# Weights asked for later, and a planner with one wire and other durations, in a three-layer decoder kernel

## The reference, cut to what matters

```
x = x + local(layernorm(x))             # 16 heads; a token sees its 7 nearest neighbours
x = x + cross(layernorm(x), ctx_1024)   # 16 heads; softmax over 120 context rows
h = layernorm(x)
h = h + causal(rmsnorm(h, n1_w))        # 16 heads, causal mask
h = h + silu(rmsnorm(h, n2_w) @ up.T) @ down.T * (sum of the 2 largest gate shares, normalised)
x = x + h
```

## Time and profile before

| what | value |
|---|---|
| median of 3 runs | 3523.06 us (3519.29 to 3523.43) |
| profiled execution | 3525.48 us, its span 3523.7 us |
| mean granted TensorE clock | 0.986 of full |
| TensorE, VectorE, GpSimd, ScalarE busy | 97%, 76%, 71%, 52% of the span |
| DMA queue of SP | 217.44 MB, 18.0% of 16 engines' span |

### The profile page before, as it was taken

The page is one execution under the profiler, slowest core; times in us unless marked ns, Lnnn a source line. Parts: engine busy times, 40 slices in busy tenths (PEclk is TensorE's granted clock), DMA queues, the critical chain, the costliest instruction groups (busy, mean ns, idle before and its releaser), DMA issues.

```text
span 3523.7 us, 91852 instructions
## 1 busy us (share of the span) xinstructions
PE 3421.1 (97%) x36229; PEld 2775.1 (79%) x36229; DVE 2680.4 (76%) x5867; ACT 1829.9 (52%) x4241; POOL 2499.1 (71%) x3160
## 2 busy tenths in 40 slices
PE   5699999999999999999999999999999999999997
PEld 4477888888888888888888888888888888888876
DVE  5687787787787787787787787787787787787763
ACT  2345545545545545545545545545545545545542
POOL 5677777777777777777777777777777777777731
PEclk8799999999999999999999999999999999999998
DMA  5111221121121221121121221221121121121200
GB/s 169 61 52 47 69 77 47 69 77 47 69 77 47 69 77 47 69 77 47 69 77 47 69 77 46 69 77 47 69 77 47 69 77 47 69 77 47 69 8 10
DMA packets 90149, 223.31 MB, mean 63 GB/s; under 512 B 9286, under 2 KB 56706, under 8 KB 73346
## 3 DMA queue, kind: packets, MB, share of 16 engines
q1 hardware_dynamic: 89730, 217.44, 18.0%
HBM read 164.92 MB, written 50.39 MB: 61 GB/s over the span
## 4 chain that ended last, share of the span: by engine, by line
PE 95%; DVE 2%; ACT 1%; POOL 1%; DMA 0%; issue 0%; SPq 0%; DVEq 0%; ACTq 0%
PE ps L892 13%; PE ps L901 13%; PE ps L763 11%; PE ps L870 10%; PE ps L819 10%; PE ps L741 9%; PE ps L797 9%; PE ps L842 8%; PE ps L769 4%; PE ps L721 3%; PE ps L791 1%; PE ps L808 1%; PE ps L856 1%; ACT prob L1006 1%; DVE nmax L1328 1%; DMA y<-in_ctx 0%
## 5 line engine op out<-in xcount | busy, mean ns | idle before, releaser
L1162 POOL TENSOR_TENSOR chunks<-v_windows,xT 128x560 f32<-128x560 f32 (+1 forms) x384 | 880.0, 2302 | 85.5 <-DVE xT L1303 76.6
L1328 DVE TENSOR_REDUCE nmax<-ps 128x4 f32<-128x480 f32 (+2 forms) x1280 | 776.8, 671 | 178.0 <-PE ps L797 178.0
L1006 ACT ACTIVATE prob<-ps 128x256 f32<-128x256 f32 (+2 forms) x1536 | 670.5, 557 | 436.0 <-PE ps L819 436.0
L1157 POOL TENSOR_TENSOR chunks<-rest,k_windows 128x512 f32<-128x512 f32 (+1 forms) x384 | 552.2, 1454 | 366.7 <-DMA k_windows<-passed_on 291.7
L1282 DVE TENSOR_REDUCE held<-chunks 128x80 f32<-128x560 f32 (+1 forms) x384 | 294.4, 767 | 303.3 <-POOL chunks L1162 297.0
L892 PE MATMUL ps<-xT,w_up 128*128 128x256 f32 x2048 | 485.2, 385 | 1.6 <-ACT xT L959 1.6
L901 PE MATMUL ps<-w_down,held 128*128 128x256 f32 x2048 | 459.0, 382 | 1.9 <-DVE held L1381 1.6
L901 PEld LDWEIGHTS ps<-w_down,held 128*128 128x128 f32 x2048 | 383.9, 190 | 59.7 <-DVE held L1381 1.9
L892 PEld LDWEIGHTS ps<-xT,w_up 128*128 128x128 f32 x2048 | 375.2, 191 | 70.5 <-issue 20.2
L959 ACT COPY xT<-ps 128x512 f32<-128x512 f32 x256 | 153.1, 598 | 355.1 <-PE ps L721 355.1
L1174 POOL TENSOR_SCALAR_AFFINE_SELECT prob<-prob 128x512 f32<-128x512 f32 x512 | 310.9, 641 | 35.9 <-ACT prob L1006 35.8
(11 more groups left out here) (150 smaller groups left out, 6719.6 us busy)
## 6 DMA issues: line engine op xcount, KB each, us to landing
k_windows<-passed_on SPq DMA_DIRECT2D x64, 1024.0 KB, 5.0
v_windows<-passed_on SPq DMA_DIRECT2D x64, 1024.0 KB, 5.0
x<-in_x SPq DMA_DIRECT2D x64, 256.0 KB, 2.9
passed_on<-rest SPq DMA_DIRECT2D x64, 256.0 KB, 2.0
passed_on<-held SPq DMA_DIRECT2D x64, 256.0 KB, 3.4
out<-x SPq DMA_DIRECT2D x64, 256.0 KB, 2.2
y<-in_ctx SPq DMA_DIRECT2D x64, 120.0 KB, 2.8
held<-nmaxT SPq DMA_DIRECT2D x256, 8.0 KB
```

The costliest lines, as they stand in the source:

```text
L1006: last = nc.scalar.activation(prob_pair(seq, L, m)[0:keys, :, r, col:col + qs], of_pair, ACT.Exp, scale=SCALE)
L1157: last = nc.gpsimd.tensor_tensor(chunk_of(c).rearrange("p (j d) -> p j d", d=D), q_row, window("k", (b + first) * D, (D, n), (1, D)), ALU. ...
L1162: last = nc.gpsimd.tensor_tensor(chunk_of(c).rearrange("p (h i j) -> p h i j", i=HD, j=WINDOW), window("v", b * D + first * HD, (HD, n), ( ...
L1328: nc.vector.tensor_reduce(of_heads[:, ms[0]:ms[-1] + 1, :, r], src, AX_X, ALU.max, negate=True).then_inc(emptied[b], 1)
```

## The change

- `setup_parts` gives transfers their bytes (`kb`), and the plan keeps one `wire` on which transfers follow each other at 330 KB/us, each seen 1.1 us (`LANDING`) after it has passed.
- Many durations and lags in the plan are other numbers (ACT and DVE lag 0.15 to 0.2, `derive bias` 4.6 to 7.0, `window_max` 1.68 to 1.38, and so on). TensorE's parts take up to twice as long in the plan after a pause of over 1.5 (`warmth`). A PSUM bank is empty 0.24 after its reader, whichever engine that is.
- `BEHIND`: group 3 is offered to SP only when the first sequence's k fetch has been issued, group 4 when its v fetch has been.
- GpSimd's masks become a part of the plan (`constants`), with the same instructions.
- `EARLY` and `EARLY_ON_DVE` would let VectorE do some of the multiplications of the first sequences. `EARLY` is 0, so no part uses it, and no such instruction is emitted.

`POSITION`, `SHIFTED`, `FILLING`, `LOOKS` and all emitted instructions stay. The core of the diff:

```
-LAG = {"PE": 0.21, "ACT": 0.15, "DVE": 0.15, "POOL": 0.1}
+LAG = {"SP": 1.1, "PE": 0.21, "ACT": 0.2, "DVE": 0.2, "POOL": 0.1}
-DIVIDE, REJOIN, CHANGE = 0.1, 0.2, 0.11
+DIVIDE, REJOIN, CHANGE = 0.1, 0.22, 0.15
+EASY_REJOIN = 0.13
+WIRE = 330.0
+LANDING = 1.1
+COOLS_AFTER, WARMS_IN = 1.5, 3.4
+EMPTIED = 0.24
+EARLY = 0
+BEHIND = {("weights", (3,), "SP"): ("fetch", ("k",), "SP", 0), ("weights", (4,), "SP"): ("fetch", ("v",), "SP", 0)}
...
-             for n, (busy, lag) in enumerate(((2.0, 5.0), (2.0, 6.0), (3.0, 10.0), (4.5, 12.0), (5.5, 18.0)))]
-    part("zeros", (), "SP", 0.6, [], lag=2.5)
+             for n, (busy, kb) in enumerate(((1.9, 768), (1.9, 768), (2.8, 1280), (3.5, 1040), (4.0, 2060)))]
+    part("zeros", (), "SP", 1.2, [], lag=LANDING, kb=60)
+    constants = part("constants", (), "POOL", 5.1, [])
...
-    part("derive", ("bias",), "DVE", 4.6, [loads[3], ("derive", ("half",), "DVE")])
+    part("derive", ("bias",), "DVE", 7.0, [loads[3], ("derive", ("half",), "DVE")])
     part("derive", ("scale",), "DVE", 4.3, [loads[3], loads[4]])
...
-    loaded = part("load", (), "SP", 2 * DMA_ISSUE, [], [("lane", ())], lag=3.2)
+    loaded = part("load", (), "SP", 2 * DMA_ISSUE, [], [("lane", ())], lag=LANDING, kb=376)
-                    sent[w] = part("send", (w,), "SP", DMA_ISSUE, [rows[w]], lag=1.9)
+                    sent[w] = part("send", (w,), "SP", DMA_ISSUE, [rows[w]], lag=LANDING, kb=256)
-                fetched[w] = part("fetch", (w,), "SP", DMA_ISSUE, [sent[w]], [(w + "_window", ())], lag=4.8)
+                fetched[w] = part("fetch", (w,), "SP", DMA_ISSUE, [sent[w]], [(w + "_window", ())], lag=LANDING, kb=1024)
...
+                        if now - stopped > COOLS_AFTER:
+                            warmth = 0.0
+                        cold = min(2 * (end - now), WARMS_IN - warmth)
+                        warmth += cold
+                        end += cold / 2
+                        stopped = end
+                    landed = end
+                    if p.kb:
+                        wire = landed = max(wire, end) + p.kb / WIRE
...
+                    j = released.get((n, i))
+                    if j is not None:
+                        missing[0, j] -= 1
+                        if not missing[0, j]:
+                            offer(0, j)
```

More of the change, by code:

```diff
@@ L62, in score_units @@
     return fills if layer == CROSS else fills + [tuple((g, 1) for g in range(4))]
-Part = namedtuple("Part", "name args engine busy lag after takes gives")
-LAG = {"PE": 0.21, "ACT": 0.15, "DVE": 0.15, "POOL": 0.1}
+Part = namedtuple("Part", "name args engine busy lag after takes gives kb", defaults=(0,))
+LAG = {"SP": 1.1, "PE": 0.21, "ACT": 0.2, "DVE": 0.2, "POOL": 0.1}
 DMA_ISSUE = 0.42
@@ L162, in sequence_parts, with part @@
     needs.update({("up", m): needs["up", 0] for m in range(1, 4)})
-    def part(name, args, engine, busy, after, takes=(), gives=(), lag=None):
+    def part(name, args, engine, busy, after, takes=(), gives=(), lag=None, kb=0):
         first = engine in ("PE", "SP")
@@ L231, in sequence_parts @@
                 held.append(a)
-                a = part(*step, "ACT", 2.0 if u < 2 else 2.3, [a] + first[1::2], (), [("quad", step)])
+                a = part(*step, "ACT", 1.95 if u < 2 else 2.15, [a] + first[1::2], (), [("quad", step)])
                 held.append(a)
@@ L299, in __init__, with engine_of @@
         at = {p[:3]: i for i, p in enumerate(parts)}
+        early = {i: EARLY_ON_DVE[p[:2]] for i, p in enumerate(parts) if p[:2] in EARLY_ON_DVE and p.engine == "POOL"}
+        released = {(who[3], at[who[:3]]): at[what] for what, who in BEHIND.items()}
+        def engine_of(n, i):
+            return "DVE" if n < EARLY and i in early else parts[i].engine
         followers = defaultdict(list)
@@ L323, in offer @@
         def offer(n, i):
-            if parts[i].engine != "PE":
-                ready[parts[i].engine].append((n + due[i] + 0.001 * n, n, i))
-                ready[parts[i].engine].sort()
+            e = engine_of(n, i)
+            if e != "PE":
+                ready[e].append((n + due[i] + 0.001 * n, n, i))
+                ready[e].sort()
+        for i in released.values():
+            missing[0, i] += 1
         for n, i in todo:
-            if not parts[i].after:
+            if not missing[n, i]:
                 offer(n, i)
@@ L366, in __init__ @@
         idle, events, now = set(engines), {}, 0.0
+        wire, stopped, warmth = 0.0, 0.0, 0.0
         while True:
@@ L385, in __init__ @@
                     self.order[e].append((p.name, n, p.args))
-                    end = now + p.busy
+                    busy = early[i] if e == "DVE" and i in early else p.busy
+                    end = now + busy
                     if e == "PE":
@@ L1051, in _ @@
[L1051 to L1065, removed]
@@ L1273, in _ @@
                         w, b, first, n = CHUNKS[c]
-                        dve.wait_ge(multiplied[s], reached["multiplied", "window_times", seq, (c,)])
+                        if seq < EARLY and ("window_times", (c,)) in EARLY_ON_DVE:
+                            dve.wait_ge(doubled[s], reached["doubled", "window_times", seq, (c,)])
+                        else:
+                            dve.wait_ge(multiplied[s], reached["multiplied", "window_times", seq, (c,)])
                         if w == "k":
```

151 lines of the change are left out of this document (94 added, 57 removed).

## The result

The changed kernel took 3541.52 us, the median of 4 runs (3539.04 to 3548.05), against 3523.24 (4 runs) for the kernel before. The ratio is 1.0047, 95% interval 1.0034 to 1.0059: slower by 0.5%, where 3511 was forecast, and outside the range. The profiled execution is the longest of the four, 3548.05 us with a span of 3546.3, so its 22.6 us over the span before overstate the median's 18.3.

The account below looks back on a forecast made before the run. TensorE was taken as the bound, saturated in the middle, with losses in the ramp set by the first sequence's local attention. First sequence -10 and rest of the ramp -2 gave -12 us: 3511 us against the median, range 3490 to 3531.

Parts of the forecast that it names:

- Start of the first k chunk: First sequence's first k chunk, at 31.58 before: starts near 27.5 through earlier `project_rows` and send, -4 us.
- rival 1: Ramp: wire and VectorE give the gain back, sends land no earlier; 3521 us, chance 0.20.
- Chunk stalls: First sequence's k chunks: two of three GpSimd stalls go, the one of `bias` stays, -5.5 us.
- Softmax: First sequence, from last k chunk to first v chunk: a little less lost, -0.5 us, bounds -1.4 and +3.
- scale: VectorE's 7.2 us weight scaling, expected at k's end or in the softmax: 0 us, bounds -3.7 and +3.5.
- the first sequence: Sum of the terms up to the first sequence's turn: -10 us, turn near 65.5.
- The rest of the ramp: Ramp after the first sequence's turn: same chain 10 us earlier, a further -2 us, bounds -12 and +8.
- One of my own signs: Ramp check: if the turn is early but TensorE's idle in 0 to 200 isn't less, a later sequence sets the ramp.
- The drain: End of the kernel: may reorder, 0 us, within 3, a tenth of 29 us idle.
- The middle: Strict middle: TensorE's order unchanged, other engines may differ; 0 us, bounds -2 and +15.
- my threshold of 398: Middle, 400 to 800 us: TensorE busy below 398 would show a stall per sequence at work.
- rival 3: Middle: one wrongly ordered pair stalls TensorE each sequence; 3540 us at 0.5 us per sequence, chance 0.14.

Follow-up runs that it names:

- e1_behind_only: The kernel before with only the held-back weight groups (`BEHIND`) added, old durations and no wire: 3516.77 us, 0.9977 of the kernel before.
- e11: The changed kernel with wire, bytes, SP's durations and `BEHIND` kept, but old durations, lags and bank times for all other engines: 3515.82 us.
- e6: The changed kernel planned with new durations until TensorE's line reaches sequence 8, old ones from there, `BEHIND` kept: 3527.45 us.
- e9: The changed kernel with TensorE forbidden to take `down` out of turn anywhere: 3521.05 us, 0.9992 of the kernel before.
- e10: The changed kernel with TensorE forbidden to take `down` out of turn at the end only: 3528.82 us, 1.0014 of the kernel before.
- e4: The changed kernel with `BEHIND` empty, so the weights are offered freely again: 3540.20 us, 1.0048 of the kernel before.
- e3: The changed kernel with no look-ahead for TensorE at the end: 3534.27 us, 1.0030 of the kernel before.

## Why the prediction was wrong, step by step

- **Start of the first k chunk: -4 forecast, -1.7 measured** (29.90 for 31.58). The order came as forecast: `project_rows` at 11.82 for 12.5, the send issued at 17.43 for 16.9. But the send took 7.5 us, so the fetch went out at 24.96, later than the 24.12 of before. The count of 4,756 KB ahead stood in the text; what failed was landing the send "near 21.5". With as many bytes ahead, asking 3.6 us sooner bought nothing: it is rival 1's mechanism, and `e1_behind_only` confirms it, whose send goes out at 21.02 and whose first chunk starts at 29.85 all the same. The other half held: the fetch met only the send, and the first chunk started 4.9 us after its issue, for 7.5 before. The 1,040 KB of group 3, issued right behind it, cost it nothing, where an even share would have cost up to 3.5.
- **Chunk stalls: -5.5 forecast, -6.0 measured** (29.90 to 44.32 is 14.4 us for 20.4). `bias` stayed where forecast, and the other two stalls went. Right.
- **Softmax: -0.5 forecast, +2.7 measured.** From 44.32 to 52.57 are 8.25 us, inside its bound of +3. `window_sum` could start once ScalarE had done its exponential, at 49.28, and started at 51.05, since VectorE's queue had a `project_rows` in front that waited 2.88 us for TensorE. This is the profiled execution's value: in the three others with the same ramp order the gap is 5.60, 6.41 and 7.43 us, so between 0 and +1.9.
- **`scale`: 0 forecast, -0.3 measured** from the first v chunk to the turn. It still holds GpSimd (3.08 us for 3.74). It came neither at the end of k nor into the softmax, as I had it, but behind the softmax (from 52.32), as in the kernel before.
- So **the first sequence**: -10 forecast, -5.3 measured, the turn at 70.20 for 65.5 (-5.1 to -8.0 over the four executions of this order). By itself this mis-sized sum would have left a forecast of about 3516.
- **"*The rest of the ramp.* From there the chain is the same"**: this step failed. It was priced at -2, bounds -12 and +8, and of the 5.3 us gained at the turn 2.6 are left at the store of sequence 0; at that of sequence 3 the kernel is 7.4 us behind. So 12.7 us were given back in the profiled execution, and 9.4 to 10.3 in the three others with this order. One of my own signs said so: the turn is early and the idle of 0 to 200 is 70.7 us, not less than 70.3, so a later sequence sets the ramp. TensorE's order isn't the same: it differs in 173 of 2433 places, in sequences 0 to 6 and 60 to 63. I argued that TensorE's work wouldn't become the bound. It needn't: a worse order alone does it. e11 and e6 show that the new durations of the engines made it, and e9 that barring early `down`s takes 7.8 us of it away. Which single durations did it stays open.
- **The drain: "0, within 3"**: failed, +10.4. The size I took was a tenth of the 29 us that TensorE idles in the end of the ramp and the drain. But a reordering isn't bounded by the present idle time: here it opened a gap of 5.14 us where there was none, with a granted clock of 0.59 behind it. e10 takes this term away with 19 places of order.
- **The middle: 0, within -2 and +15**: right in kind. TensorE, ScalarE, GpSimd and SP keep their orders there, VectorE's differs in 151 places from sequence 8 to 58, and it costs some 2 us (+0.5 to +2.5 in the other kernels with the new durations there, +4.8 in the profiled execution of the changed kernel). The stretch from 400 to 800 has 398.13 us, only just above my threshold of 398, but 4.8 us over 55 sequences are 0.09 each, less than half of the 0.2 from which rival 3, a stall per sequence, would have taken the gain. So it isn't the cause.

What remains of the sum: by profile, ramp +2 to +7.4, middle +1.6 to +4.8, drain +10.4, which is 14 to 23 us, and the medians differ by 18.3. None of my rivals was this one. Rival 3 had the right doubt ("`POSITION` and `SHIFTED` are untouched while durations changed") and put it in the one place where TensorE may not choose.

Why truer durations made worse orders is only partly settled. The runs show that barring `down`, 7 us that nothing interrupts, from going early gains 12.7 us at the end and 7.8 more in the ramp, with the places that shift behind it. What makes the plan take it early can be read from the planner alone, which is no measurement: at the early `down`s of sequences 0, 60, 61 and 62 the `scores` at the head of the line have all their inputs, and what they lack is a free half of the PSUM banks. With the ScalarE and VectorE lags alone set back to 0.15, the three `down`s at the end are still early in the plan; with the bank times alone set back, `down` of sequence 62 returns to its place. Neither plan was run on the chip. Not tried either: new offsets (`POSITION`, `SHIFTED`) for the new durations, and single durations one by one. Which early `down` costs what in the ramp is open too.

## What to carry to other kernels

When the change touches numbers that feed a greedy scheduler, compare the emitted orders first, and put the doubt where the scheduler may choose: here TensorE's order in the strict middle couldn't move, while the fill went from -8.5 (e1) to +7.4 and the drain from -3.3 (e10) to +10.4. A long part that is ready was not a good filler when the part at the head could start soon and had a chain behind it; forbidding that one choice was worth 12.7 us at the end. And the send that was issued 3.6 us earlier gained nothing behind as many bytes: count the bytes ahead, and let that set the landing. Last, look at more than one execution before a term of the ramp is called measured: one order gave softmax gaps from 5.60 to 8.25 us.

## What the runs showed of the hardware that I had not expected

- A send of 256 KB took 7.5 us from issue to use with some 4.7 MB asked for ahead of it, against a median of 2.1 us to landing for this form on the page after.
- The issue of `w_gate`'s load alone held SP's queue for 4.79 us, where the loads of `w_up` and `w_down` before it take 0.43 and 0.47. It isn't a fixed price of this load: in e4, which asks for it at 22.33, the same issue takes 1.90 us, in e3 6.47. Why isn't shown.
- VectorE's scaling of `w_up` and `w_gate` took 4 and 9 times as long while GpSimd multiplied chunks (52.57 to 57.68): the same form on the same shapes took 3.10 and 0.74 us, 2.11 and 0.23. It isn't that the first of two is slow: in e11, where GpSimd multiplies nothing from 45.13 to 53.42, the first `w_up` at 45.21 takes 0.75 and the first `w_gate` 0.23.

```profile
52.58 3.10 DVE L1290 TENSOR_SCALAR w_up<-w_up,scale 128x1024 f32<-128x1024 f32 x1
55.61 2.11 DVE L1290 TENSOR_SCALAR w_gate<-w_gate,scale 128x32 f32<-128x32 f32 x1
...
57.90 0.74 DVE L1290 TENSOR_SCALAR w_up<-w_up,scale 128x1024 f32<-128x1024 f32 x1
58.56 0.23 DVE L1290 TENSOR_SCALAR w_gate<-w_gate,scale 128x32 f32<-128x32 f32 x1
```

- One and the same order of all engines in the ramp reached the store of sequence 3 at 392.8 to 398.3 us in four executions, 5.4 us apart, while the middle of the seven other kernels that share its orders there spans 2.0 (+0.5 to +2.5, and +4.8 in the profiled execution of the changed kernel). One profiled ramp tells no smaller difference than 5 us.
